# Edge lists scattered by GpSimd, the mix block moved ahead, row sums in three groups of relations

## The chip, the cores and the metric

One Trainium2 chip; the kernel runs on one core of it. The metric is the device time of one execution in microseconds (us), as the median of several runs. Engines are named PE (TensorE), DVE (VectorE), ACT (ScalarE), POOL (GpSimd) and SP (SyncE).

## The reference, cut to what matters

```python
# x [1250,1024], 20000 edges (src, dst, type in 0..7), dst sorted; all fp32
xn  = layernorm(x)
u   = xn @ root + bias
for r in range(8):                       # relational graph convolution
    sums = segment_sum(xn[src] * (type == r), dst)
    u   += (sums / max(count_r, 1)) @ weight[r]
z   = concat([u, xn]) @ w_gate + b_gate
h   = tanh(u) * z + xn * (1 - z)
mix = taylor_linear_attention(rms_norm(xn), w_q, w_kv) @ w_out     # 8 heads of 16
x   = x + h + mix
x   = x + fp4_ffn(layernorm(x))          # 1024 -> 352 -> 1024, fp4 in blocks of 16
```

## The kernel before

Rows are cut into NT = 10 tiles of 128. PE first multiplies all rows with all weights of the graph stage: 21 column blocks h (one of 384 columns for q, k, v; 16 blocks of 512 for the eight relations, two each; two for root; two for the lower half of w_gate) times 10 tiles, so NSTEP = 210 **steps** n = 10h + t. A step is `product(n)`: eight slices k of 128 input columns, three matmuls each (fp32 is made of a high and a low part, XTH/XTL and WH/WL). The finished block goes through ACT (`evacuate`, from PSUM into the tile EV) to device memory. `product` calls `beside(n, k)` after each slice k, and there everything else that PE does is placed by step number: the edge lists, the attention (mix), the summing of rows. The same step numbers place the work on the other engines, whose queues run in program order, so an instruction that waits holds up all that stands behind it on its engine. GpSimd's part in each step is `low_rows` (eight of ten steps: WL = RAW - WH, for the column block after this one; PE waits for it at the first step of a block) and then its DMAs.

A relation's result for node v is a weighted sum over v's incoming edges of rows xn[src] @ weight[r], that is of rows that `product` has stored (`relation_rows`). These rows are fetched with GpSimd's indirect DMA, 128 rows (one **item**) at a time, into a ring of four slots, and summed per tile of 128 destination nodes:

- A **plane** item holds at most one edge per destination node, so it is already aligned: DVE adds it to the sum with one SCALAR_TENSOR_TENSOR of 128x1024 (`plane`).
- A **left-over** item holds the edges that did not fit into the planes. ACT makes the high part (`left_over_hi`), DVE a one-hot matrix and the low part (`left_over`), and PE adds it with four matmuls of 512 columns (`aggregate`), in the step after the item's own, behind its last slice where the step has one such item. Only then is its slot free again.
- `finish` adds PE's sum and DVE's sum; SP stores it in u_rows (`store_sum`) and, for a later group, loads it again (`load_sum`).

Relations are taken in groups, each of which can start once its relations are multiplied. Before: group 0 is relations 0 to 4 (8 planes and 3 left-over items per tile, from step 117), group 1 is relations 5 to 7 (5 planes and 2 left-over items, from step 178). That is 180 items, 50 of them left-over.

The **lists** say which row each slot of an item holds. DVE computes a place for every edge (`edge_words`, `edge_places`, until step 19). Then for each of the 160 columns of 125 edges DVE makes three one-hot matrices and ACT two, and PE multiplies them (`list_column`, three fp16 matmuls), four columns in each of the steps 20 to 59. DVE turns the result into row numbers and weights (`list_results`).

The mix block: keys and values at steps 64 to 83 (`key_heads`; its features are made half by DVE and half by POOL, `key_features`), queries at steps 85 to 115 (`query_t`, `query_heads`, `attention_t`, `mix`). Beside steps 118 to 173 DVE quantizes the feed-forward weights (24 calls of `quantize`, three in seven steps). After step 209 come the gate matmuls and the feed-forward part. If the edges do not fit (`count_rounds`), everything is summed again in rounds (`more_rounds`).

Of the kernel before, what the change touches and what calls it, by code (L numbers as in the profile page):

```python
# [8 lines left out]
ALU = mybir.AluOpType  # L9
ACT = mybir.ActivationFunctionType  # L10
# [7 lines left out]
P = 128  # L18
N = 1250
D = 1024  # L20
# [15 lines left out]
GROUPS = ((0, 5), (5, R))  # L36
NG = len(GROUPS)
PLANES = (8, 5)
OVER = (3, 2)
# [6 lines left out]
GCB = (11, 7)  # L46
# [3 lines left out]
SW = NCOL + 2  # L50
# [42 lines left out]
LIST_FROM, LIST_EACH = 20, 4  # L93
TOTALS_AT = 76
KEYS_FROM = 64
QUERIES_FROM, QUERIES_EACH = 85, 3
AGG_FROM = (117, 178, NSTEP)
# [60 lines left out]
def gps_layer(nc, x, src, dst, edge_type_8, weight, root, bias, w_gate, b_gate, gamma, w_q, w_kv,  # L158
              w_out, ff_gate, ff_up, ff_down, out):
    with ExitStack() as ctx:  # L160
# [6 lines left out]
        def stage_tensors(*specs):  # L167
# [8 lines left out]
        qkv_d = nc.dram_tensor("qkv_rows", [NP, 3 * HID], F32).ap()  # L176
        z_d = nc.dram_tensor("gate_x_rows", [NP, D], F32).ap()
# [17 lines left out]
        iota1 = keep("iota1", [P, P], F16)  # L195
        zeros16 = keep("zeros16", [P, P], F16)
# [23 lines left out]
        unfit = keep("unfit", [P, 1], F32)  # L220
        rounds = keep("rounds", [1, 1], I32)
# [45 lines left out]
        US0, US1, XD, ZD, MD, US2 = stage_tensors(  # L267
            ("u_tile0", [P, D], F32), ("u_tile1", [P, D], F32), ("x_tile", [P, 2, D], F32),
            ("z_tile", [P, 2, D], F32), ("mix_tile", [P, 2, D], F32), ("u_tile2", [P, D], F32))
# [41 lines left out]
        dve_e = [sem(f"dve_e{j}") for j in range(5)]  # L311
# [6 lines left out]
        dve_f = [sem(f"dve_f{j}") for j in range(4)]  # L318
# [3 lines left out]
        words_ready = sem("words_ready")  # L322
        oh_dve = sem("oh_dve")
# [11 lines left out]
        f_dve = sem("f_dve")  # L335
        f_pool = sem("f_pool")
# [42 lines left out]
        pool_d = sem("pool_d")  # L379
# [18 lines left out]
        pool_x = sem("pool_x")  # L398
# [21 lines left out]
        XN = [a[:, 0:D] for a in (flat_a, flat_b)]  # L420

# [132 lines left out]
        def more_rounds(eng, body, first=None):  # L554
# [26 lines left out]
        def _(sp):  # L581
# [84 lines left out]
            for n in range(NSTEP + 1):  # L666
# [1561 lines left out]
```

## Time and profile before

| | us |
|---|---|
| median of 3 runs (lowest to highest) | 1745.39 (1743.96 to 1749.13) |
| profiled execution, its own time | 1751.03 |
| span of the profiled execution | 1749.3 |
| PE busy | 1633.5 (93%) |
| DVE busy | 995.0 (57%) |
| POOL busy | 613.0 (35%) |
| ACT busy | 498.8 (29%) |
| mean granted TensorE clock | 0.977 |

The busy time of PE is that of its matmuls, whose recorded ends overlap the next start. Idle time of the other engines costs something only where PE waits for them.

### The profile page before, as it was taken

What the parts mean: (1) busy time and instruction counts of PE and PEld (TensorE: products, weight loads), DVE (VectorE), ACT (ScalarE), POOL (GpSimd) and SP (SyncE); (2) the same over time, 40 slices, a digit from 0 to 9 for tenths busy, and PEclk for the clock granted to TensorE, in tenths of its full rate; (3) what the DMA queues carried; (4) which work ended last, traced back from release to release, by engine and by line L of the source; (5) the groups of instructions that cost most, each with busy time, mean ns of one, the idle gap of its engine ahead of it and who ended that gap; (6) DMA issues with size and microseconds to landing.
All of it is one profiled execution on the core that took longest, in us unless ns stands there. A gap on an engine that the chain in (4) does not pass through costs nothing.

```text
span 1749.3 us, 20493 instructions
## 1 busy us (share of the span) xinstructions
PE 1633.5 (93%) x7618; PEld 1290.5 (74%) x7618; DVE 995.0 (57%) x1709; ACT 498.8 (29%) x901; POOL 613.0 (35%) x523
## 2 busy tenths in 40 slices
PE   4999999999999999999999999999899869977988
PEld 4987777777777666667788787878677658866887
DVE  6544555552111433332878878884567745777885
ACT  3325555551111121212222222222211122232221
POOL 4321111124665110103555455545655641220110
PEclk8999999999999999999999999999999979987999
DMA  4321122222222222224778677777888774540001
GB/s 150 130 94 67 68 77 73 72 74 99 80 87 96 72 95 88 100 77 145 238 260 275 223 250 269 256 247 242 294 281 301 274 250 144 181 133 1 37 37 46
DMA packets 114963, 261.57 MB, mean 150 GB/s; under 512 B 18203, under 2 KB 31634, under 8 KB 114856
## 3 DMA queue, kind: packets, MB, share of 16 engines
q1 hardware_dynamic: 48568, 109.34, 18.5%
q0 software_dynamic: 27552, 82.01, 14.5%
q10 hardware_dynamic: 38736, 68.83, 10.4%
q8 instruction: 62, 1.02, 0.2%
q14 instruction: 45, 0.37, 0.1%
HBM read 192.96 MB, written 79.61 MB: 156 GB/s over the span
## 4 chain that ended last, share of the span: by engine, by line
PE 66%; DVE 16%; DMA 8%; issue 5%; ACT 3%; POOL 1%; ACTq 0%; SPq 0%; DVEq 0%; POOLq 0%
PE ps L1657 47%; DMA source_rows<-relation_rows,row_list 6%; PE ps L1872 5%; PE ps L1745 3%; DVE u_sum L1416 2%; PE ps L1904 2%; PE ps L1765 2%; PE ps L1922 1%; DVE source_rows L1400 1%; PE ps L1725 1%; DMA u_sum<-u_rows 1%; PE ps L1757 1%; ACT source_rows_hi L2048 1%; DVE wq_rows L546 1%; PE ps L1705 1%
## 5 line engine op out<-in xcount | busy, mean ns | idle before, releaser
L1657 PE MATMUL ps<-WH,XTH 128*128 128x512 f32 (+1 forms) x1680 | 681.7, 406 | 0.0
L1657 PE MATMUL ps<-WH,XTL 128*128 128x512 f32 (+1 forms) x1680 | 654.3, 389 | 0.0
L1657 PE MATMUL ps<-WL,XTH 128*128 128x512 f32 (+1 forms) x1680 | 653.7, 389 | 0.0
L814 POOL TENSOR_TENSOR WL<-RAW,WH 128x512 fp32r<-128x512 f32 (+1 forms) x184 | 241.3, 1315 | 559.9 <-ACT WH L1981 557.8
L1657 PEld LDWEIGHTS ps<-WH,XTH 128*128 128x128 f32 x1680 | 317.9, 189 | 78.1 <-issue 22.5
L1657 PEld LDWEIGHTS ps<-WH,XTL 128*128 128x128 f32 x1680 | 316.9, 189 | 65.6
L1657 PEld LDWEIGHTS ps<-WL,XTH 128*128 128x128 f32 x1680 | 318.3, 189 | 57.1 <-issue 2.4
L866 POOL DMA_INDIRECT source_rows<-relation_rows,row_list x180 | 224.2, 1245 | 263.2 <-PE ps L1765 145.2
L2003 ACT ACTIVATE EV<-ps 128x512 f32<-128x512 f32 x180 | 106.4, 591 | 452.6 <-PE ps L1657 378.1
L1416 DVE SCALAR_TENSOR_TENSOR u_sum<-source_rows,weight_list,u_sum 128x1024 f32<-128x1024 f32 x120 | 168.0, 1400 | 74.1 <-DMA source_rows<-relation_rows,row_list 67.0
L1981 ACT ACTIVATE WH<-RAW 128x512 fp32r<-128x512 f32 (+1 forms) x184 | 114.6, 624 | 140.7 <-DVE EV L1458 79.0
L1291 DVE TENSOR_SCALAR onehot<-iota,edge_words 125x128 f16<-125x128 f16 x160 | 72.1, 450 | 129.1 <-PE ps L1705 129.1
L1400 DVE SCALAR_TENSOR_TENSOR source_rows<-source_rows,weight_list,source_rows_hi 128x1024 fp32r<-128x1024 f32 x50 | 85.3, 1705 | 75.9 <-ACT source_rows_hi L2048 75.8
L1366 DVE TENSOR_TENSOR prefix<-ps,qkv_tile 128x544 f32<-128x544 f32 x40 | 29.0, 725 | 163.1 <-PE ps L1745 163.1
L2048 ACT ACTIVATE source_rows_hi<-source_rows,weight_list 128x1024 fp32r<-128x1024 f32 x50 | 57.5, 1149 | 170.6 <-DMA source_rows<-relation_rows,row_list 152.6
L2011 ACT ACTIVATE onehot<-iota,edge_words 125x82 f16<-125x82 f16 x160 | 58.1, 363 | 111.6 <-PE ps L1705 98.7
L1872 PE MATMUL ps<-WH,TH 128*128 128x512 f32 x160 | 65.3, 408 | 10.1 <-DVE TL L1516 10.1
L2012 ACT ACTIVATE onehot<-iota,edge_words 125x182 f16<-125x182 f16 x160 | 69.1, 432 | 0.0
L950 POOL TENSOR_TENSOR xf<-xf,edge_words 128x1024 f32<-128x1024 f32 x10 | 19.4, 1942 | 138.0 <-DVE xf L1566 138.0
L1350 DVE COPY values<-qkv_tile 128x128 f32<-128x128 f32 x10 | 2.4, 241 | 113.4 <-PE ps L1729 113.4
L1872 PE MATMUL ps<-WL,TH 128*128 128x512 f32 x160 | 64.2, 401 | 0.0
L1872 PE MATMUL ps<-WH,TL 128*128 128x512 f32 x160 | 64.1, 401 | 0.0
(299 smaller groups left out, 1868.8 us busy)
## 6 DMA issues: line engine op xcount, KB each, us to landing
relation_rows<-EV ACTq DMA_DIRECT2D x160, 256.0 KB, 2.0
RAW<-in_L_gnn_weight SPq DMA_DIRECT2D x128, 256.0 KB, 2.7
u_rows<-u_sum SPq DMA_DIRECT2D x20, 512.0 KB, 5.2
RAW<-in_L_gnn_w_gate SPq DMA_DIRECT2D x32, 256.0 KB, 4.7
mix_rows<-mix_rows_out ACTq DMA_DIRECT2D x10, 512.0 KB, 2.6
root_rows<-EV ACTq DMA_DIRECT2D x20, 256.0 KB, 4.5
u_sum<-u_rows SPq DMA_DIRECT2D x10, 512.0 KB, 7.6
bias_rows<-root_rows SPq DMA_DIRECT2D x10, 512.0 KB, 7.2
```

What stands on the lines that cost most here:

```text
L814: g.tensor_tensor(WL[:, h % 2, k, 0:w], RAW[:, q % 4, 0:w], WH[:, h % 2, k, 0:w].bitcast(F32), ALU.subtract).then_inc(w_lo, 1)
L866: return g.indirect_dma_start(out=XG[:, slot, :].bitcast(F32), out_offset=None, in_=y_d[group], in_offset=bass.IndirectOffsetOnAxis(ap=row ...
L1291: v.tensor_scalar(oh_src(s), iota[0:EP, 0:P], ew[0:EP, LO, col], ew[0:EP, SRC1, col], ALU.is_equal, ALU.mult)
L1400: v.scalar_tensor_tensor(rows_, rows_.bitcast(F32), weight_list[:, m.column:m.column + 1], OHI[:].bitcast(F32), ALU.mult, ALU.subtract).th ...
L1416: v.scalar_tensor_tensor(acc[:], XG[:, m.index % RING, :].bitcast(F32), weight_list[:, m.column:m.column + 1], base[:], ALU.mult, ALU.add) ...
L1657: mm = t_.matmul(ps[:, bank, 0:w], a[:, t, k, :], b[:, s, k, 0:w], start=(k == 0 and j == 0), stop=(k == KT - 1 and j == 2))
L1872: mm = t_.matmul(ps[:, 4 + 2 * s + b, :], a[:, s, k, :], w[:, h % 2, k, :], start=(k == 0 and j == 0), stop=(k == KT - 1 and j == 2))
L1981: a.activation(WH[:, h % 2, k, 0:w], raw, ACT.Copy).then_inc(w_hi, 1)
L2003: a.activation(ev_slot(s), ps[:, prod_bank(n), :], ACT.Copy).then_inc(ev, 1)
L2011: a.activation(oh_bk(s), iota[0:EP, 0:SB], ACT.Sign, bias=ew[0:EP, BQ, col])
L2012: a.activation(oh_chunk(s), iota[0:EP, 0:SW], ACT.Sign, bias=ew[0:EP, CH, col]).then_inc(oh_act, 1)
L2048: a.activation(OHI[:], XG[:, slot, :].bitcast(F32), ACT.Copy, scale=weight_list[:, m.column:m.column + 1]).then_inc(oh_hi, 1)
```

## The change

- The one-hot lists go. DVE computes for each edge a slot number (SLOT) and a word that packs source, relation and destination (WORD), and POOL writes the words with 160 indirect DMAs (125 words of 4 bytes each) into four lists in device memory, three per step from step 19; each waits for the landing of the one four before it. At step 75 the four lists are read back; DVE adds and unpacks them (`list_results`).
- The counts of edges per node and relation come from the planes by DVE reductions, and for the left-over columns from 30 matmuls of 8 columns on PE (`count_left`, steps 79 to 82).
- DVE counts the edges of each bucket directly (`bucket_totals`: three one-hots of 125x1600 and three reductions) between the edge places and the first key tile.
- The mix block moves: keys from step 20, queries from step 41. DVE makes both halves of the key features.
- Three groups: relations 0-2, 3-5, 6-7, with 7, 7, 5 planes and 1 left-over item each per tile, from steps 91, 134 and 174. That is 220 items, 30 of them left-over, and 30 sums instead of 20.
- Code for further rounds changes with it; it runs only if edges do not fit.

```diff
-GROUPS = ((0, 5), (5, R))
+GROUPS = ((0, 3), (3, 6), (6, R))
-PLANES = (8, 5)
-OVER = (3, 2)
+PLANES = (7, 7, 5)
+OVER = (1, 1, 1)
...
-LIST_FROM, LIST_EACH = 20, 4
-KEYS_FROM = 64
-QUERIES_FROM, QUERIES_EACH = 85, 3
-AGG_FROM = (117, 178, NSTEP)
+SCATTER_FROM, SCATTER_EACH = 19, 3
+KEYS_FROM = 20
+QUERIES_FROM, QUERIES_EACH = 41, 3
+LISTS_AT = 75
+COUNT_FROM = 79
+COUNTED_AT = COUNT_FROM - (-NOV // KT) + 2
+AGG_FROM = (91, 134, 174, NSTEP)
...
+            def scatter(c):
+
+                k = c % NLIST
+                pool.wait_ge(listed[k], 16 * (c // NLIST + 1))
+                g.indirect_dma_start(
+                    out=list_d[k], out_offset=bass.IndirectOffsetOnAxis(
+                        ap=ew[0:EP, SLOT, c:c + 1].bitcast(U32), axis=0),
+                    in_=ew[0:EP, WORD, c:c + 1].bitcast(I32), in_offset=None,
+                    bounds_check=P * NCOL - 1, oob_is_err=False).then_inc(listed[k], 16)
...
-                i, odd = divmod(n - KEYS_FROM, 2)
-                if 0 <= i < NT and not odd:
-                    pool.wait_ge(vt_ready, i + 1)
-                    key_features(g, i % 2, 1, f_pool)
+                if n == SCATTER_FROM:
+                    pool.wait_ge(words_ready, 1)
+                if n >= SCATTER_FROM:
+                    for c in range(c_next, min(c_next + SCATTER_EACH, EC)):
+                        scatter(c)
...
             edge_words()
             edge_places()
-            for c in range(EC):
-                list_column(c, c % 4, slice(c, c + 1), True)
-            list_results()
+            bucket_totals()
...
-                key_features(v, s, 0, f_dve)
+                for half in range(2):
+                    key_features(v, s, half, f_ready[half])
...
-                if 0 <= n - LIST_FROM < EC // LIST_EACH and k % 2 == 1:
-                    c = LIST_EACH * (n - LIST_FROM) + k // 2
-                    list_column(c, c % 4, True)
+                q = KT * (n - COUNT_FROM) + k
+                if 0 <= q < NOV:
+                    count_left(q)
```

How the change moves instructions, at three places. **PE, step 20** (WH, WL, XTH, XTL are the products' operands; onehot of L1701 to L1705 are the list's one-hots). Before, from the second slice of the step:

```order
L1657 MATMUL ps<-WL,XTH 128x512
L1657 MATMUL ps<-WH,XTL 128x512
L1701 MATMUL ps<-onehot 128x82
L1703 MATMUL ps<-onehot 128x182
L1705 MATMUL ps<-onehot 128x182
L1657 MATMUL ps<-WH,XTH 128x512
```

In the changed kernel, at the fifth slice of the same step (onehot is here the buffer with the first half of the key features):

```order
L1749 MATMUL ps<-WH,XTH 128x512
L1749 MATMUL ps<-WL,XTH 128x512
L1749 MATMUL ps<-WH,XTL 128x512
L1832 MATMUL ps<-onehot,qkv_tile 32x289 x4
L1749 MATMUL ps<-WH,XTH 128x512
```

The list's three matmuls are gone from the slices, and the first matmuls of the key heads stand in this step instead of step 64.

**DVE, behind the edge places.** Before, the last words and the first list column:

```order
L1126 TENSOR_TENSOR prefix<-prefix 125x160
L1127 TENSOR_TENSOR prefix<-prefix 125x160
L1128 TENSOR_SCALAR edge_words<-prefix 125x160
L1291 TENSOR_SCALAR onehot<-iota,edge_words 125x128
L1294 TENSOR_SCALAR onehot<-iota,edge_words 125x128
L1295 TENSOR_SCALAR onehot<-iota,edge_words 125x128
```

In the changed kernel, from the word that GpSimd waits for (L1180) to the first half of the first key tile (L440, L442):

```order
L1180 SCALAR_TENSOR_TENSOR edge_words<-prefix,unsorted 125x160
L1066 TENSOR_SCALAR edge_words<-edge_words 125x160
L1069 SCALAR_TENSOR_TENSOR edge_words<-edge_words 125x160
L1311 TENSOR_TENSOR edge_words<-edge_words 125x160
L1303 TENSOR_TENSOR onehot<-edge_words,bucket_ids 125x1600
L1314 TENSOR_REDUCE edge_totals<-onehot 125x10
L1303 TENSOR_TENSOR onehot<-edge_words,bucket_ids 125x1600
L1314 TENSOR_REDUCE edge_totals<-onehot 125x10
L1303 TENSOR_TENSOR onehot<-edge_words,bucket_ids 125x1600
L1314 TENSOR_REDUCE edge_totals<-onehot 125x10
L1438 COPY values<-qkv_tile 128x8x16
L1439 COPY values<-valid 128x8
```

The three large one-hots and their reductions stand before the key tile that PE wants in step 20.

**GpSimd, between the low halves of the weights (WL).** Before, where the 51 rows of the low halves in a run span the list stage:

```order
L855 MEMSET weight_list 128x180
L814 TENSOR_TENSOR WL<-RAW,WH 128x512 x51
L894 DMA edge_weights<-rcnt 128x80
L859 DMA weight_list<-edge_weights,weight_at 128x1 x2
L814 TENSOR_TENSOR WL<-RAW,WH 128x512
```

In the changed kernel (L829 is the low half, L908 the scatter):

```order
L872 MEMSET weight_list 128x220
L875 DMA edge_lists<-weight_list 128x220 x4
L829 TENSOR_TENSOR WL<-RAW,WH 128x512 x16
L908 DMA edge_lists<-edge_words 28160x1 x6
L829 TENSOR_TENSOR WL<-RAW,WH 128x512
L908 DMA edge_lists<-edge_words 28160x1 x3
L829 TENSOR_TENSOR WL<-RAW,WH 128x512
```

From here on three scatters stand ahead of each low half, until the 160 are done.

## Rows read from the trace of the kernel before

**Rows 1.** The page: span, busy time, the chain that ended last.
```profile
span 1749.3 us, 20493 instructions
PE 1633.5 (93%) x7618; PEld 1290.5 (74%) x7618; DVE 995.0 (57%) x1709; ACT 498.8 (29%) x901; POOL 613.0 (35%) x523
PE 66%; DVE 16%; DMA 8%; issue 5%; ACT 3%; POOL 1%; ACTq 0%; SPq 0%; DVEq 0%; POOLq 0%
```

**Rows 2.** Waits of PE: who waited for whom, us in total, times, longest.
```profile
PE ps L1765 <- DVE source_rows L1400: 30.7, 20, 3.1
```

**Rows 3.** Busy time by stretch: lists, keys, queries, both groups of sums, the rest.
```profile
core 0: us, PE busy (x) PEld busy (x) DVE busy (x) ACT busy (x) POOL busy (x), PEclk, DMA share, GB/s
136.10:397.40 261.30, 261.30 (x1443) 189.64 (x1441) 130.96 (x468) 145.51 (x384) 41.41 (x32) 1.00 0.21 74
419.70:558.20 138.50, 138.50 (x666) 99.47 (x665) 21.38 (x46) 22.08 (x36) 89.00 (x78) 1.00 0.23 78
569.20:812.90 243.70, 240.51 (x940) 166.92 (x939) 91.91 (x162) 48.66 (x83) 36.18 (x30) 1.00 0.24 86
818.40:1194.60 376.20, 364.58 (x1585) 299.02 (x1584) 296.44 (x389) 99.72 (x140) 203.00 (x161) 0.99 0.76 253
1194.60:1411.80 217.20, 198.10 (x846) 159.93 (x845) 143.38 (x124) 44.91 (x58) 121.00 (x93) 0.98 0.80 277
1411.80:1749.30 337.50, 280.46 (x1407) 243.86 (x1405) 231.05 (x321) 85.72 (x113) 60.35 (x40) 0.92 0.28 100
```

**Rows 4.** Timeline of ACT: evacuations of neighbouring steps (start, length): plain, list, left-over.
```profile
408.80 0.60 ACT L2003 ACTIVATE EV<-ps 128x512 f32<-128x512 f32 x1 [3.75 <-PE ps L1657]
414.24 0.60 ACT L2003 ACTIVATE EV<-ps 128x512 f32<-128x512 f32 x1 [3.75 <-PE ps L1657]
...
255.04 0.58 ACT L2003 ACTIVATE EV<-ps 128x512 f32<-128x512 f32 x1
261.57 0.58 ACT L2003 ACTIVATE EV<-ps 128x512 f32<-128x512 f32 x1
...
1015.72 0.60 ACT L2003 ACTIVATE EV<-ps 128x512 f32<-128x512 f32 x1 [1.88 <-PE ps L1657]
1022.07 0.60 ACT L2003 ACTIVATE EV<-ps 128x512 f32<-128x512 f32 x1 [1.48 <-PE ps L1657]
```

**Rows 5.** Timeline of PE: first matmul of step 20.
```profile
136.08 0.48 PE L1657 MATMUL ps<-WH,XTH 128*128 128x512 f32 x1
```

**Rows 6.** Timeline of DVE, edge places: carry from PE to last word, and a key tile.
```profile
116.78 0.16 DVE L1077 COPY run_carry<-ps 125x2 f32<-125x2 f32 x1 [4.80 <-PE ps L1680]
116.98 0.99 DVE L1079 TENSOR_TENSOR_SCAN prefix<-prefix,run_carry 125x160 f32<-125x160 f32 x2
118.53 0.51 DVE L1083 TENSOR_REDUCE edge_words<-prefix 125x160 f32<-125x320 f32 x1
129.09 0.24 DVE L1128 TENSOR_SCALAR edge_words<-prefix 125x160 f32<-125x160 f32 x1
...
432.20 1.29 DVE L427 TENSOR_TENSOR onehot<-qkv_tile,values 128x1088 f32<-128x1088 f32 x1
...
596.57 1.12 DVE L1368 TENSOR_REDUCE prefix<-prefix 128x34 f32<-128x544 f32 x1
```

**Rows 7.** Lines L859 (weights) and L866 (rows): indirect DMAs of GpSimd.
```profile
L859 POOL DMA_INDIRECT weight_list<-edge_weights,weight_at x50: 996/1010/2023, 421.1 to 583.8; - x50
  issue: 11.2, 46
DMA to landing us min/median/max: 2.2/2.5/4.5
...
L866 POOL DMA_INDIRECT source_rows<-relation_rows,row_list x180: 987/1072/2035, 816.0 to 1407.4; - x180
DMA to landing us min/median/max: 3.4/6.2/9.5
```

**Rows 8.** Lines of POOL, 136 to 560: busy, mean ns, idle before.
```profile
L814 POOL TENSOR_TENSOR WL<-RAW,WH 128x512 fp32r<-128x512 f32 x51 | 65.8, 1291 | 277.2 <-ACT WH L1981 277.1
```

**Rows 9.** Lines of DVE, first group of sums: busy, mean ns, idle before.
```profile
L1416 DVE SCALAR_TENSOR_TENSOR u_sum<-source_rows,weight_list,u_sum 128x1024 f32<-128x1024 f32 x70 | 95.4, 1363 | 29.5 <-DMA source_rows<-relation_rows,row_list 26.0
L1400 DVE SCALAR_TENSOR_TENSOR source_rows<-source_rows,weight_list,source_rows_hi 128x1024 fp32r<-128x1024 f32 x30 | 49.8, 1661 | 46.1 <-ACT source_rows_hi L2048 46.0
...
L1396 DVE TENSOR_SCALAR edge_one_hots<-iota,key_list 128x128 fp32r<-128x128 f16 x30 | 12.6, 420 | 0.2
L1426 DVE TENSOR_TENSOR u_sum<-ps,u_sum 128x1024 f32<-128x1024 f32 x9 | 10.9, 1215 | 0.0
```

More of the change, by code:

```diff
@@ L322, in gps_layer @@
         words_ready = sem("words_ready")
+        listed = [sem(f"listed{k}") for k in range(NLIST)]
+        lists_in = sem("lists_in")
+        left_ready = sem("left_ready")
+        left_used = sem("left_used")
+        left_ps = sem("left_ps")
         oh_dve = sem("oh_dve")
@@ L334, in gps_layer @@
         vt_ready = sem("vt_ready")
-        f_dve = sem("f_dve")
-        f_pool = sem("f_pool")
+        f_ready = [sem(f"f_ready{half}") for half in range(2)]
         key_done = sem("key_done")
@@ new lines, in edge_places @@
+                v.scalar_tensor_tensor(T(1), T(1), float(NCOL), T(3), ALU.mult, ALU.add)
+                ch.step(v.scalar_tensor_tensor(T(5), eword(BK), float(2 ** 20), T(5), ALU.mult, ALU.add))
+                v.tensor_copy(eword(WORD).bitcast(I32), T(4))
+                v.scalar_tensor_tensor(eword(SLOT).bitcast(U32), T(1), unsorted[0:EP, 1:2], T(5), ALU.add,
+                                       ALU.add).then_inc(words_ready, 1)
+            def list_results():
+                dve.wait_ge(lists_in, 16 * NLIST)
+                ch = edge_chain
+                low, high = 4 * P + NOV * R // 2, NLIST * NCOL
+                word, src, rel, key = [flat_b[:, low + NCOL * j:low + NCOL * (j + 1)] for j in range(4)]
+                none, tmp, tmp1 = [flat_a[:, high + NCOL * j:high + NCOL * (j + 1)] for j in range(3)]
+                ints = lambda w: w.bitcast(I32)
+                left = slice(NPL, NCOL)
@@ L1169, in list_results @@
                 planes = lambda w, j: w[:, PLANE0[j]:PLANE0[j] + NT * PLANES[j]].rearrange(
                     "p (t c) -> p t c", t=NT)
+                lefts = lambda j: slice(OVER0[j], OVER0[j] + NT * OVER[j])
+                group = lambda r: max(j for j in range(NG) if r >= GROUPS[j][0])
+                flat = LISTS.rearrange("p k c -> p (k c)")
+                ch.step(v.tensor_copy(flat.bitcast(F32), flat))
+                ch.step(v.tensor_reduce(word, LISTS.bitcast(F32).rearrange("p k c -> p c k"), AX.X, ALU.add))
@@ new lines, in list_results @@
+                for q in range(NOV):
+                    need(dve, left_used, q - 7)
+                    v.tensor_scalar(LEFT16[:, q % 8, :], iota1[:], key_list[:, q:q + 1], None,
+                                    ALU.is_equal).then_inc(left_ready, 1)
+                ch.step(v.tensor_scalar(none, none, 65536.0, None, ALU.mult))
+                v.tensor_tensor(src, src, none, ALU.add)
+                ch.step(v.scalar_tensor_tensor(key[:, left], key[:, left], float(NB), none[:, left], ALU.mult,
+                                               ALU.add))
@@ new lines, in list_results @@
+                ch.step(v.scalar_tensor_tensor(tmp1[:, left], rel[:, left], float(NT), key[:, left], ALU.mult,
+                                               ALU.add))
+                ch.step(v.tensor_tensor(weight_at[:], tmp1[:, left], tmp[:, left], ALU.add))
+                for r in range(R):
+                    j, same = group(r), (tmp, tmp1)[r % 2]
+                    ch.step(v.tensor_scalar(planes(same, j), planes(rel, j), float(r), None, ALU.is_equal))
+                    counted = v.tensor_reduce(rcnt[:, NT * r:NT * r + NT], planes(same, j), AX.X, ALU.add)
@@ L1672, in run_ends_t @@
                 pe.wait_ge(run_ready, 2 * level + 1)
+                if level == 0:
+                    pe.wait_ge(consts, NCONST)
+                    t_.matmul(ps[0:EP, 0, 3 * P:3 * P + 1], ones[0:EP, 0:EP], unsorted[0:EP, 0:1], start=True,
+                              stop=True)
                 t_.transpose(ps[0:NG, 0, 0:EP], run_ends[0:EP, 0:NG], ident[0:EP, 0:EP])
```

338 lines of the change are left out of this document (194 added, 144 removed).

## Prediction

> **What bounds the kernel now.** I read the page first, then the waits of PE, then busy time by stretch, then single lines. PE is busy 93% of the span and carries 66% of the chain that ended last [rows 1]; the reader is to see that no other engine comes near. PE's waits in the steps are few: the one large row is PE waiting for the low part of a left-over item, 30.7 us over 20 waits [rows 2]. So the question is how much work leaves PE's queue, and which new waits come in.
>
> The unit is the step. A plain one takes 5.44 us (evacuations at 408.80 and 414.24), one with four list columns 6.53 (255.04, 261.57), one with one left-over item 6.35 (1015.72, 1022.07) [rows 4]. By stretch: the 40 list steps take 261.3 us, the 20 key steps 138.5, the 30 query steps 243.7, steps 117 to 177 (first group of sums, 61 steps, 30 left-over items) 376.2, steps 178 to 209 (second group, 32 steps, 20 left-over items) 217.2, and all behind step 209 takes 337.5 [rows 3]. The granted clock is 1.00 up to step 115, 0.99 and 0.98 in the sums, 0.92 in the rest [rows 3]; I leave it as it is.
>
> How much the sums cost in waits: 61 plain steps are 331.8 us and 30 items at 0.91 are 27.3, which leaves 376.2 - 359.1 = 17.1 us of waiting in the first group; 32 x 5.44 + 20 x 0.91 = 192.3 leaves 24.9 us in the second. Together 42.0; rows 2 has 30.7 of it, as a wait begins in the trace only when the modelled end of the matmul before is past.
>
> **The change, part by part.**
>
> *Lists off PE.* 40 steps x (6.53 - 5.44) = -43.6 us. They stand on PE's path, and nothing but PE's own work fills these steps: PE is busy for all of the 261.3 us [rows 3].
>
> *Fewer left-over items.* 20 fewer x 0.91 = -18.2 us.
>
> *The old waits in the sums go*: -42.0, and new ones are counted below.
>
> *Mix moved.* The same matmuls in other steps: the key stretch costs 1.4 us a step above a plain one before, and will now; 0. DVE makes both halves: 1.29 us more per tile [rows 6] in a pair of steps of 13.8; hidden, except at the first tile.
>
> *The first key tile.* PE wants it behind the fifth slice of step 20. That step starts at 136.1 [rows 5], and 5/8 of 5.44 later is 139.5. DVE's side: the carry comes at 116.8, when PE reaches its place, and the last word is ready at 129.3, 12.5 us later [rows 6]. The third group adds a third scan (0.49), four more dependent operations of about 0.35 in the places, and longer products and reductions; I count 3.9 us: words at 133.2. Then `bucket_totals`: about 1 us of small operations and three pairs of a one-hot of 1600 elements and its reduction. No row has this size. A TENSOR_TENSOR of 1088 takes 1.29 us, so about 1.8 for 1600; a reduction of 320 takes 0.51, so also about 1.8 [rows 6]. Three pairs are 11.1 us: 145.3. The values and the first half take 2 us more: 147.3. PE waits 147.3 - 139.5 = +8 us, once; later tiles have a pair of steps each. Bounds: the other reduction row, 544 elements in 1.12 us [rows 6], makes three of 1600 slower by some 4 us, and with delays of 1 us by GpSimd's traffic it is 15; if my count of added operations is twice too large, 4. I take 8, as the 320-element row is contiguous like the new one.
>
> *Counting matmuls.* 30 of 8 columns. Three list matmuls with 446 columns cost (6.53 - 5.44) / 4 = 0.27 us; one tiny one lies between 0 and 0.27. I take a third, 0.09: +2.7 (0 to 8).
>
> *GpSimd's scatters.* 160 indirect DMAs, three a step from step 19 to 72. The nearest is the weight fetch, 128 words of 4 bytes: 1.01 us, with 0.24 of issue before it, landed after 2.5 (at most 4.5) [rows 7]. Each scatter waits for the fourth before it; four take 4 x 1.3 = 5.2 us, so the landing is past. Queued behind each is the low half of the weights, for which PE waits at the first step of a block. GpSimd's need over the 20 key steps is 16 x 1.29 [rows 8] + 60 x 1.3 = 99 of 138 us; over the 30 query steps 24 x 1.29 + 90 x 1.3 = 148 of 244. Hidden: 0. The lists come back at step 75, the first counting matmul is at step 79, 22 us later; the four loads (about 5 us) and some ten DVE operations before it fit.
>
> *The new sums.* Work per group as DVE must do it, at 1.36 us a plane, 1.66 + 0.42 a left-over item, 1.22 a `finish` [rows 9]. For a `quantize` I take what is left of DVE's 296.4 us in the first group [rows 3] when 80 planes (95.4 and ten more at 1.37), 49.8, 12.6 and 10.9 [rows 9] are off: 114 / 24 = 4.75 us.
> - Group 0, steps 91 to 133: PE's own time 43 x 5.44 + 9.1 = 243; DVE 95 + 21 + 12 + 6 x 4.75 = 157. Slack, but steps 91 to 99 give GpSimd two weight fetches beside two row fetches and a low half, 6 us in steps of 5.44, and the ring is cleared at its start. I take +10 (2 to 20).
> - Group 1, steps 134 to 173: PE's own time 227; DVE 95 + 21 + 12 + 18 x 4.75 = 214, which is 94%, where the first group before ran at 296.4 / 376.2 = 79% and lost 17 us in 61 steps. Low end 5, as if the rate fell with the fewer left-over items. High end: DVE's idle time of the first group, 79.8 us for 110 items or 0.73 each, stays; 214 + 58 = 272, so 45. I take +17, nearer the low end, since much of that idle time was DVE being ahead of PE.
> - Group 2, steps 174 to 209: PE's own time 205. One left-over item per 3.6 steps instead of two per 3.2. A left-over item's slot is free only when PE has added it, and the next fetch, 6.2 us to its landing and up to 9.5 [rows 7], hangs on that; before, the second of a tile blocked the first of the next. DVE has 68 + 21 + 24 + 14 for evacuations = 127. I take +4 (0 to 15).
>
> That is +31 (7 to 80). Twenty more stores and loads of sums are on SP; each load is issued two steps (group 2: 1.2) ahead of its use, and DVE, which waits for it, has the slack above; within the terms.
>
> Sum: -43.6 - 18.2 - 42.0 + 8 + 2.7 + 31 = -62 us. Against the profiled execution's own 1751.0 it gives 1689. That execution is 5.6 above the median of the runs, 1745.4, so I forecast **1683**. With all low ends it is 1745.4 - 103.8 + 11 = 1653, with all high ends 1745.4 - 103.8 + 103 = 1745.
>
> **The rivals.**
>
> *DVE becomes the bound in group 1.* For it: 94% of the stretch, and three blocks of 4.75 us in seven steps between items whose fetches want a free slot. Against it: the slack of an item is its own step and the next, about 11 us, more than one block. Group 1 then loses 45 instead of 17 and group 0 some 9 more: 1683 + 37 = 1720.
>
> *The waits nearly vanish.* For it: each fetch now moves 20000 / 220 = 91 rows instead of 111, the short left-over ones land near the least time of 3.4 us [rows 7], and one left-over item per tile frees the ring. Then the sums lose about 12 instead of 31: 1664. Against it: the quantizing beside group 1 and the first key tile remain.
>
> *The scatters hold GpSimd up (slower).* The mechanism: a scatter that takes longer than its share delays the low halves behind it, and PE stands at each tenth step from 20 to 72. The point from which it decides: keys 20.6 + 60p against 138, queries 31 + 90p against 244, so nothing is lost up to a pitch p of 1.95 us; at 2.34 (the longest of the 230 fetches, 2.04, with its issue) 23 us are lost, which leaves 1706; the whole gain is gone at 2.6; at 3.0 the loss is 120, so 1803. For it: no row shows an indirect write, and DVE works beside it all the time. Against it: the weight fetches ran beside DVE's key features and the median stayed at 1.01 us [rows 7]. The Trainium skill ("SBUF — State Buffer", "Who interferes with whom") has a rule that speaks for this rival: a DVE copy or one-scalar operation in its two-port mode holds the port pair that GpSimd needs to write descriptors, and by its section on the bandwidth-pool intuition a DMA of 0.62 us took 3.1 us beside one. By that figure as a pitch the time would be above 1803. The trace agrees only so far as single fetches take 2.02 and 2.04 us instead of 1.0 [rows 7].
>
> *It does not do what it says.* If one bucket had more left-over edges than its 128 places, a whole further round would run. Counting the reference's edges gives at most 104 in a bucket (tile 7, relations 0-2) and 87 and 65 in the other groups, so this is out. That something else keeps the order of work from moving gives 1745.
>
> **How the numbers follow.** Forecast 0.62 (its own range 1670 to 1702); DVE bound 0.17; waits vanish 0.12; scatters 0.05, of which 0.03 end slower; unchanged for any reason 0.02; slower by a loss in a place that I have not seen 0.02. The range takes in the two rivals beside the forecast up to the cut: 1658 to 1716. Within 0.3% (5 us, about what a measurement of this kernel can tell from no change) 0.02; slower 0.03 + 0.02 = 0.05; faster 0.62 + 0.17 + 0.12 + 0.02 = 0.93.
>
> **What would show it.** Right: steps 20 to 59 without 6.53 us ones outside keys and queries; one wait of PE for the first half of the key features, near 8 us, in step 20; the last product's end near 1350 (1411.8 - 62); between it and the end of the span again 337 us; row waits of PE for the low part shorter in group 2 than in group 1. Wrong: waits of PE for WL in the first half (scatters); indirect writes with a mean over 1.6 us; a stretch of steps 134 to 173 above 260 us (DVE bound); waits of PE at steps 79 to 82 for the counting one-hots; or a longer stretch behind step 209.

## The result, and the profile after

The changed kernel takes **1717.84 us** (median of 4 runs, 1716.05 to 1721.86) against 1745.18 (4 runs, 1743.96 to 1749.13): ratio 0.9843 [0.9819, 0.9867]. It is faster by 27 us where 62 were forecast, and 2 us above the range.

The page after, to be read against [rows 1]:

```profile
span 1714.3 us, 19015 instructions
PE 1576.8 (92%) x7088; PEld 1265.8 (74%) x7088; DVE 967.8 (56%) x1352; ACT 372.3 (22%) x561; POOL 823.1 (48%) x693
PE 58%; DVE 22%; DMA 8%; issue 6%; ACT 3%; POOL 3%; ACTq 0%; SPq 0%; POOLq 0%; DVEq 0%
```

PE's busy time fell by 57 us, the span by only 35, and PE's share of the chain went from 66% to 58%: work was exchanged for waits. The waits of PE after, against [rows 2] (who waited for whom: us in total, times, longest):

```profile
PE ps L1872 <- DVE source_rows L1490: 44.2, 12, 10.0
PE ps L1832 <- DVE onehot L442: 6.7, 1, 6.7
PE ps L1749 <- POOL WL L829: 2.6, 1, 2.6
```

The large row is still the left-over item's low part, but it stands for 12 long waits instead of 20 short ones. The windows after, against the last three of [rows 3]: steps 90 to 132, steps 133 to 173 (group 1 starts at 134), group 2 to the last product, the rest:

```profile
640.30:894.60 254.30, 246.26 (x1073) 202.42 (x1072) 157.30 (x155) 57.19 (x87) 164.90 (x134) 0.99 0.70 226
894.60:1152.10 257.50, 238.85 (x1026) 195.54 (x1026) 213.81 (x272) 56.41 (x85) 142.38 (x114) 0.97 0.78 259
1152.10:1381.40 229.30, 209.18 (x905) 171.75 (x903) 136.23 (x120) 38.89 (x56) 118.83 (x91) 0.96 0.72 239
1381.40:1714.30 332.90, 276.58 (x1403) 240.52 (x1402) 228.50 (x318) 85.44 (x113) 63.34 (x40) 0.92 0.27 98
```

The last product ends at 1381.4 (1411.8 before; 1350 was forecast), and 332.9 us follow. To find the rest I took the start of every step from the trace of PE and subtracted 5.44 us, and 0.91 for a left-over item; what remains is waiting, and with it the slower products behind a wait. (From 91 on it is 61.0 us where the rows of waits have 46.8: behind the wait of 10.0 us, for example, the four matmuls of the left-over item took 1.85 us instead of 0.91.) In this table the first column is the length of step 20 (a key step with no wait is 6.95), the next five are waits by steps, and "end" is that of the last product. The lower rows are experiments, told below.

| | step 20 | 91-116 | 117-133 | 134-173 | 174-177 | 178-209 | end |
|---|---|---|---|---|---|---|---|
| after | 15.9 | 6.8 | 4.5 | 25.3 | 2.7 | 21.7 | 1381.4 |
| forecast | about 15 | 10 with the next | | 17 | 4 with the next | | 1350 |
| E1 root rows without the wait | 15.4 | 8.9 | 7.1 | 22.5 | 6.1 | 0.4 | 1364.7 |
| E2 group 2 from 178 | 15.6 | 8.4 | 7.7 | 20.9 | 0.0 | 10.0 | 1366.8 |
| E3 two groups | 7.6 | 0.0 | 1.1 | 12.3 | 0.7 | 25.2 | 1372.5 |
| E4 no quantizing | 15.4 | 8.3 | 0.0 | 0.2 | 0.0 | 18.1 | 1346.2 |
| E5 changed kernel again | 15.9 | 8.9 | 7.7 | 23.5 | 5.3 | 21.0 | 1386.4 |
| E6 totals late | 7.0 | 8.5 | 4.5 | 22.9 | 5.2 | 18.8 | 1371.9 |
| E7 four weight fetches a step | 16.1 | 11.9 | 5.5 | 26.4 | 5.4 | 22.1 | 1392.3 |
| E8 four edits | 7.0 | 16.8 | 0.0 | 1.4 | 0.0 | 8.2 | 1337.8 |
| E9 groups from 95, 136, 178 | 7.0 | 6.9 | 2.8 | 2.3 | 0.1 | 10.2 | 1333.2 |
| E10 groups from 91, 134, 178 | 7.0 | 8.8 | 1.7 | 0.0 | 0.0 | 9.7 | 1331.5 |
| E11 two groups, mended | 7.0 | 0.3 | 0.0 | 0.0 | 0.0 | 22.5 | 1354.8 |
| E12 weights later | 7.0 | 0.0 | 2.3 | 0.0 | 0.1 | 13.0 | 1326.7 |
| E13 E10 again | 7.0 | 12.0 | 2.3 | 0.0 | 0.0 | 9.9 | 1335.5 |

**The first key tile.** ACT's evacuations of steps 19 and 20, 16.15 us apart, as [rows 4] are read, then DVE in between and PE's wait:

```profile
135.39 0.60 ACT L2120 ACTIVATE EV<-ps 128x512 f32<-128x512 f32 x1 [4.84 <-PE ps L1749]
151.54 0.60 ACT L2120 ACTIVATE EV<-ps 128x512 f32<-128x512 f32 x1 [15.55 <-PE ps L1749]
```

```profile
131.27 0.38 DVE L1180 SCALAR_TENSOR_TENSOR edge_words<-prefix,unsorted 125x160 uint32<-125x160 f32 x1
132.56 1.82 DVE L1303 TENSOR_TENSOR onehot<-edge_words,bucket_ids 125x1600 f32<-125x1600 f32 x1
134.41 1.82 DVE L1314 TENSOR_REDUCE edge_totals<-onehot 125x10 f32<-125x1600 f32 x1
...
145.60 0.19 DVE L442 COPY onehot<-values 128x68 f32<-128x68 f32 x1
```

```profile
138.76 0.39 PE L1749 MATMUL ps<-WH,XTL 128*128 128x512 f32 x1
145.85 2.15 PE L1832 MATMUL ps<-onehot,qkv_tile 128*32 128x289 f32 x8 [6.70 <-DVE onehot L442]
...
148.52 0.63 PE L1749 MATMUL ps<-WL,XTH 128*128 128x512 f32 x1
```

The one-hots and reductions of 1600 take 1.82 us each, as [rows 6] had let me estimate. PE stands 6.7 us, and the products behind it run slower at first (0.63 us, 0.39 ahead of it), so the step is 9.0 us longer than without the wait (E6).

**The scatters.** Line L908: least, median and longest in ns, then the idle time before it.

```profile
L908 POOL DMA_INDIRECT edge_lists<-edge_words x160: 1185/1190/2897, 132.7 to 542.0; - x160
...
  issue: 43.9, 144
  DMA edge_lists<-edge_words: 4.6, 16
...
DMA to landing us min/median/max: 2.5/2.7/5.5
```

With 197.1 us for 160, the mean is 1.23, and 0.3 of issue stands before each: a pitch of 1.5 us, below the 1.95 from which it decides. PE waited for no low half beside the scatters: its one such wait, the 2.6 us above, ends at 704.05 us, in step 100, and the last scatter began at 542.0. Steps 40 to 71 took 254.8 us, as their work did before (254.7 in steps 84 to 115).

**Group 2.** Here is what the prediction did not look at. SP's queue (issues of DMAs: start, length), then the wait behind the gap (the same row of before was 17.1 us, once):

```profile
1172.05 0.43 SPq L679 DMA_DIRECT2D u_rows<-u_sum  x1
1197.59 0.33 SPq L670 DMA_DIRECT2D bias_rows<-root_rows  x1
...
1198.91 0.43 SPq L675 DMA_DIRECT2D u_sum<-u_rows  x1
...
1220.68 0.33 SPq L670 DMA_DIRECT2D bias_rows<-root_rows  x1
```

```profile
SPq L669 <- DMA root_rows<-EV: 43.1, 2, 25.0
```

DVE's queue in the same time:

```profile
1181.59 1.22 DVE L1516 TENSOR_TENSOR u_sum<-ps,u_sum 128x1024 f32<-128x1024 f32 x1
1201.01 1.22 DVE L1521 TENSOR_TENSOR u_sum<-u_sum,bias_rows 128x1024 f32<-128x1024 f32 x1 [18.20 <-DMA bias_rows<-root_rows]
1205.35 5.45 DVE L1506 SCALAR_TENSOR_TENSOR u_sum<-source_rows,weight_list,u_sum 128x1024 f32<-128x1024 f32 x4 [3.12 <-DMA u_sum<-u_rows]
...
1225.20 1.23 DVE L1521 TENSOR_TENSOR u_sum<-u_sum,bias_rows 128x1024 f32<-128x1024 f32 x1 [8.49 <-DMA bias_rows<-root_rows]
```

And GpSimd's next row fetch, which wants a slot that DVE has read:

```profile
1207.40 1.49 POOL L887 DMA_INDIRECT source_rows<-relation_rows,row_list  x1 [20.38 <-DVE u_sum L1506]
```

In group 2 each tile's sum also gets its root rows (`load_root`), and these are products too: the second half of tile t's is made in step 180 + t. Group 2 now starts at step 174, so the load of its first tile stands in SP's queue at step 175, five steps before its data are made; SP reaches it at 1172.5 us, in step 177. SP stands 25.0 us, with the load of the next sum queued behind; DVE stands 18.20 and 3.12; GpSimd fetches nothing for 20.38; PE then loses 11.1 us in step 182.

The loss comes again for the second tile. PE had made its root rows in time (step 181 ends at 1200.1), but ACT stores them, and in ACT's queue their evacuation stands behind the high part of a left-over item, whose rows come late because GpSimd stood:

```profile
1213.11 1.15 ACT L2163 ACTIVATE source_rows_hi<-source_rows,weight_list 128x1024 fp32r<-128x1024 f32 x1 [16.56 <-DMA source_rows<-relation_rows,row_list]
1214.16 0.58 ACT L2120 ACTIVATE EV<-ps 128x512 f32<-128x512 f32 x1
1214.77 0.33 ACTq L2122 DMA_DIRECT2D root_rows<-EV  x1
```

So step 181 was evacuated at 1214.16 instead of right behind its end, SP could load its rows only at 1220.68, and DVE stood 8.49 again; PE lost 8.8 us in step 185.

### The profile page after: what moved, and what is told of

The parts are those of the page before. It is cut to its first block, busy times and chain, and to the rows that moved or that the text cites. A ratio compares the mean times of both kernels' runs of the same rounds, so it can differ in the third digit from the quotient of the medians.

```text
span 1714.3 us, 19015 instructions
## 1 busy us (share of the span) xinstructions
PE 1576.8 (92%) x7088; PEld 1265.8 (74%) x7088; DVE 967.8 (56%) x1352; ACT 372.3 (22%) x561; POOL 823.1 (48%) x693
## 3 DMA queue, kind: packets, MB, share of 16 engines
q1 hardware_dynamic: 51448, 119.83, 20.9%
## 4 chain that ended last, share of the span: by engine, by line
PE 58%; DVE 22%; DMA 8%; issue 6%; ACT 3%; POOL 3%; ACTq 0%; SPq 0%; POOLq 0%; DVEq 0%
PE ps L1749 42%; DMA source_rows<-relation_rows,row_list 5%; PE ps L1988 5%; DVE u_sum L1506 4%; PE ps L1852 3%; PE ps L2020 2%; PE ps L1832 1%; PE ps L1872 1%; DVE wq_rows L561 1%; PE ps L2038 1%; DVE wq_tmp L551 1%; DVE source_rows L1490 1%; PE ps L1864 1%; DVE wq_rows L562 1%; POOL source_rows L887 1%
## 5 line engine op out<-in xcount | busy, mean ns | idle before, releaser
L1749 PE MATMUL ps<-WH,XTH 128*128 128x512 f32 (+1 forms) x1680 | 670.6, 399 | 2.6 <-POOL WL L829 2.6
L887 POOL DMA_INDIRECT source_rows<-relation_rows,row_list x220 | 270.3, 1229 | 298.0 <-DVE u_sum L1506 145.0
L829 POOL TENSOR_TENSOR WL<-RAW,WH 128x512 fp32r<-128x512 f32 (+1 forms) x184 | 243.8, 1329 | 244.3 <-ACT WH L2098 241.6
L1506 DVE SCALAR_TENSOR_TENSOR u_sum<-source_rows,weight_list,u_sum 128x1024 f32<-128x1024 f32 x180 | 257.5, 1431 | 125.9 <-DMA source_rows<-relation_rows,row_list 104.8
L908 POOL DMA_INDIRECT edge_lists<-edge_words x160 | 197.1, 1232 | 48.5 <-issue 43.9
L1490 DVE SCALAR_TENSOR_TENSOR source_rows<-source_rows,weight_list,source_rows_hi 128x1024 fp32r<-128x1024 f32 x30 | 50.2, 1673 | 89.8 <-ACT source_rows_hi L2163 89.8
L1872 PE MATMUL ps<-source_rows_hi,edge_one_hots 128*128 128x512 f32 x60 | 22.0, 450 | 44.2 <-DVE source_rows L1490 44.2
L2163 ACT ACTIVATE source_rows_hi<-source_rows,weight_list 128x1024 fp32r<-128x1024 f32 x30 | 34.4, 1147 | 108.6 <-DMA source_rows<-relation_rows,row_list 102.6
L1852 PE MATMUL ps<-key_value,q_t 32*128 32x289 f32 x160 | 48.6, 422 | 3.2
```

The costliest lines, as they stand in the source:

```text
L829: g.tensor_tensor(WL[:, h % 2, k, 0:w], RAW[:, q % 4, 0:w], WH[:, h % 2, k, 0:w].bitcast(F32), ALU.subtract).then_inc(w_lo, 1)
L887: return g.indirect_dma_start(out=XG[:, slot, :].bitcast(F32), out_offset=None, in_=y_d[group], in_offset=bass.IndirectOffsetOnAxis(ap=row ...
L908: g.indirect_dma_start(out=list_d[k], out_offset=bass.IndirectOffsetOnAxis(ap=ew[0:EP, SLOT, c:c + 1].bitcast(U32), axis=0), in_=ew[0:EP, ...
L1490: v.scalar_tensor_tensor(rows_, rows_.bitcast(F32), weight_list[:, m.column:m.column + 1], OHI[:].bitcast(F32), ALU.mult, ALU.subtract).th ...
L1506: v.scalar_tensor_tensor(acc[:], XG[:, m.index % RING, :].bitcast(F32), weight_list[:, m.column:m.column + 1], base[:], ALU.mult, ALU.add) ...
L1749: mm = t_.matmul(ps[:, bank, 0:w], a[:, t, k, :], b[:, s, k, 0:w], start=(k == 0 and j == 0), stop=(k == KT - 1 and j == 2))
```

## The experiments

Ratios are against the kernel before, run beside each on the same chip. The batches are E1 to E4, E5 to E8, E9 to E11, and E12 with E13. In the diffs `...` marks lines left out.

**E1, root rows without their wait.** It adds rows of the mix in place of the root rows, so that part of the sum is other data.

```diff
-                    n = NT * (H_ROOT + b) + t
-                    sp.wait_ge(ev_out[n % 4], ev_stores(n))
-                sp.dma_start(BIASB[:], root_d[rows(t), :]).then_inc(root_in, 16)
+                    sp.wait_ge(mix_out[b], 16 * NT // 2)
+                sp.dma_start(BIASB[:], mix_d[rows(t), :]).then_inc(root_in, 16)
```

> The rows that SP loads into bias_rows for the last group are taken from mix_rows (stored since step 72) instead of root_rows; so the output leaves out the root product. Theory A (SP stands before the root rows: tile 0 of group 2 asks for them in step 175, but step 180 makes them): PE's waits in steps 174 to 209 fall from 24.5 us to under 7, and the time from 1717.8 to about 1700. Rival B (DVE comes out of group 1 too late, being 94% busy there, and the waits of group 2 are what is left of it): both stay, time 1715 to 1720.

1700.56 us, 0.9707 [0.9657, 0.9758]; 0.4 us of waits from step 178 on instead of 21.7. PE's row fell:

```profile
PE ps L1871 <- DVE source_rows L1489: 25.7, 10, 6.3
```

Group 1's waits (22.5) stayed, and so did the 6.1 us of steps 174 to 177 (5.3 in E5). So the root rows make the waits from step 178 on, and only these: of the 24.4 us that group 2 lost, some 21. The rest, at step 175, is gone in E2 and in E4.

**E2, group 2 from step 178**, with groups 0 and 1 where they were.

```diff
-AGG_FROM = (91, 134, 174, NSTEP)
+AGG_FROM = (91, 134, 178, NSTEP)
+AGG_TO = (134, 174, NSTEP)      # where the tiles of a group are spread to
...
-                step = AGG_FROM[g] + (each * t + at) * (AGG_FROM[g + 1] - AGG_FROM[g]) // (each * NT)
+                step = AGG_FROM[g] + (each * t + at) * (AGG_TO[g] - AGG_FROM[g]) // (each * NT)
```

> Group 2 (relations 6-7) starts at step 178 instead of 174; groups 0 and 1 keep their steps. Theory A: tile 0 is finished in step 181, when its root rows are there or nearly; waits of steps 174 to 209 fall from 24.5 to 8 us or less, since 60 items in 32 steps are still fewer a step than the 70 of the kernel before; time about 1701. Rival B says the same of the first waits, as DVE gets four steps to catch up, but not of e1. A third reading (the rate of the last group decides): waits as in the kernel before, 20 to 25 us, time 1718.

1703.5 us, 0.9717 [0.9668, 0.9766]: a start four steps later more than halves the loss (24.4 to 10.0, where 8 or less was expected). SP still stands 17.0 us for the first root rows, but DVE only 4.0. What the other 10 us are was not tried; 8 to 13 us stand there in every later run with three groups whose last starts at 178.

**E3, two groups**: the new lists and the moved mix alone, sums as before.

```diff
-GROUPS = ((0, 3), (3, 6), (6, R))
-PLANES = (7, 7, 5)
-OVER = (1, 1, 1)
+GROUPS = ((0, 5), (5, R))
+PLANES = (8, 5)
+OVER = (3, 2)
...
-AGG_FROM = (91, 134, 174, NSTEP)
+AGG_FROM = (117, 178, NSTEP)
```

> The new lists and the moved mix alone: two groups (0-4, 5-7) with 8 and 5 planes, 3 and 2 left-over items per tile, from steps 117 and 178, as in the kernel before. From the changed kernel's terms: 1745.2 - 43.6 (list columns) + 6 (first key tile, with one group less) + 50 x 0.15 (counting matmuls) and the sums as before, so 1715. If the three groups are worth what I forecast (more than 20 us), it is above 1725.

1712.95 us, 0.9774 [0.9729, 0.9819]. The lists and the mix give what the whole change gives (1719.27 us, 0.9823, in E5): three groups, placed as they are, were worth nothing.

**E4, no quantizing.** DVE's 24 `quantize` become a copy of 16 columns; the feed-forward part then works on unquantized weights.

```diff
-                        quantize(v, ch, WQI[:, m, :], WQT[:], WQS).then_inc(wq_done, 1)
+                        v.tensor_copy(WQT[:, 0:16], WQI[:, m, 0:16]).then_inc(wq_done, 1)
```

> DVE's 24 quantize calls become one short copy each; the feed-forward weights go through unquantized, which is the part left out. Theory A: group 1's waits (25.3 us in steps 134 to 173) fall to under 8, those of group 2 stay at 18 to 25, because SP waits for a product and not for DVE; time about 1700. Rival B: both fall, to under 8 each, time about 1683.

1685.04 us, 0.9626 [0.958, 0.9671]. Group 1's waits go from 25.3 to 0.2, those from step 178 on stay at 18.1, and DVE stands as long for the root rows:

```profile
1169.40 1.22 DVE L1521 TENSOR_TENSOR u_sum<-u_sum,bias_rows 128x1024 f32<-128x1024 f32 x1 [18.99 <-DMA bias_rows<-root_rows]
```

Two causes, then: the quantizing for group 1 and the root rows for steps 178 on. The time is 15 us below the 1700 expected and near the rival's 1683, though the rival's waits did not come out: the quantizing had also made the waits of steps 117 to 133 (4.5, 7.7 in E5) and 174 to 177 (2.7, 5.3 in E5), which are gone here.

**E5, the changed kernel again**, for comparison in its batch.

> The changed kernel itself, unedited, beside the next three on one chip. It should stand at 0.984 of the kernel before, as measured first (0.9819 to 0.9867); the other three are read against it.

1719.27 us, 0.9823 [0.9784, 0.9863]. The waits repeat within 3.2 us.

**E6, bucket totals late**: behind the last query tile, in the buffer `prefix`.

```diff
             edge_places()
-            bucket_totals()
...
                 attention(t)
+            bucket_totals()
             list_results()
```

> The bucket totals (three one-hots of 1600 elements and their reductions) move from ahead of the first key tile to behind the last query tile, where DVE waits for the lists; they use the other scratch buffer. If step 20's extra 9 us (15.9 against 6.8) is DVE's 11 us of bucket totals, step 20 falls to 7 us or so and the time by 9 us against e5. Rival (the longer chain of edge places is the cause): step 20 stays above 12 us.

1708.66 us, 0.9772 [0.9732, 0.9812]; ACT's evacuations of steps 19 and 20 are 7.18 us apart instead of 16.15:

```profile
135.79 0.60 ACT L2120 ACTIVATE EV<-ps 128x512 f32<-128x512 f32 x1 [4.84 <-PE ps L1749]
...
142.97 0.60 ACT L2120 ACTIVATE EV<-ps 128x512 f32<-128x512 f32 x1 [6.58 <-PE ps L1749]
```

**E7, four weight fetches a step** instead of two, to have them over before group 0.

```diff
-                    for q in range(w_next, min(w_next + 2, NOV)):
+                    for q in range(w_next, min(w_next + 4, NOV)):
...
-                    w_next = min(w_next + 2, NOV)
+                    w_next = min(w_next + 4, NOV)
```

> GpSimd fetches the left-over weights four a step from step 85 instead of two, so it is done at step 92 instead of 99. If the 6.8 us wait in steps 100 and 101 is GpSimd with too much to do beside the first items (two weight fetches, two row fetches and a low half in a step), it falls below 1 us, and the time by 6 us against e5. Rival (the clearing of the ring and the short lead at the start of group 0): it stays, or moves to step 93.

1724.03 us, 0.9855 [0.9817, 0.9893]. Missed: 11.9 us in steps 91 to 116, no less than in E5, now at steps 92 and 96 instead of 100.

**E8, four edits together**: group 2 from step 178, E6, E7 and a spread of the quantizing. Unlike E2, group 1 is stretched here to the start of group 2, 44 steps instead of 40; so it is in E10, E12 and E13 (E9: 42).

```diff
-AGG_FROM = (91, 134, 174, NSTEP)
-QUANT_FROM, QUANT_STEPS = 118, 7
+AGG_FROM = (91, 134, 178, NSTEP)
+QUANT_FROM, QUANT_STEPS = 92, 11
...
-in (2, 3, 5):
+in (2, 5, 8):
```

> All together: totals late (-9), four weight fetches a step (-6), group 2 from step 178 with group 1 stretched to 44 steps, and the quantize calls spread over steps 92 to 180, three in eleven steps instead of three in seven. Theory: DVE is no longer above 85% in any stretch and SP no longer stands before the root rows; waits in steps 91 to 209 fall from 61 us to 20, so together -50 against e5: about 1667. If either cause is only half of it, the time stays above 1685.

1678.33 us, 0.9598 [0.9561, 0.9635]. Group 1's waits are nearly gone (1.4), but 16.8 us stand at the start (E7 alone 11.9, E5 8.9), and the time is 11 us above the 1667 expected. E7's edit and the quantizing that now begins at step 92 were not parted there.

**E9 and E10, without E7's edit**, quantizing from step 100, three in ten steps; E9 with groups from 95, 136, 178, E10 from 91, 134, 178.

```diff
-QUANT_FROM, QUANT_STEPS = 118, 7
+QUANT_FROM, QUANT_STEPS = 100, 10
```

> As e8, but two weight fetches a step again, group 0 from step 95 (95, 136, 178) and the quantize calls from step 100, three in ten steps. Reading: the 17 us that e8 lost in steps 92 to 97 are GpSimd behind with fetches, the clearing of the ring and the first items, since e7 only moved the wait of steps 100 and 101 to 92 to 97 and made it larger. With four steps more, waits in steps 91 to 116 are under 4 us and the time is 12 us below e8: 0.953 of the kernel before. If what decides is the rate of the items (41 steps instead of 43), they stay above 8.

> As e9, but groups from steps 91, 134, 178. GpSimd's pile-up at the start as in the changed kernel: 7 to 9 us in steps 100 and 101, so 5 to 8 us above e9 and 0.956 to 0.958 of the kernel before.

E9: 1669.94 us, 0.9545 [0.9519, 0.9571]. E10: 1669.63 us, 0.9539 [0.9513, 0.9565]. The two are equal; that E10 would be slower was a miss, and so was E9's 6.9 us at the start where under 4 was expected. A start four steps later only moved the first wait, from step 100 to step 104.

**E11, two groups mended** in the same way, from 114 and 178.

> Two groups as in the kernel before (from steps 114 and 178), with the new lists, the moved mix, the late totals and the spread quantize calls: what three groups are worth once both waits are mended. PE has 20 more left-over items (18.2 us) and the old waits of the last group (25 us, one left-over item blocking the next); so 30 to 40 us above e9, 0.973 to 0.977 of the kernel before. If three groups are worth nothing, it equals e9.

1695.75 us, 0.9697 [0.9668, 0.9726]: 26 us above E9, where 30 to 40 was expected. So three groups are worth 26 us once the waits around them are mended: 20 left-over items (18.2), 12.8 less waiting in group 2 and 3 for fewer counting matmuls, against some 10 more at the start (E10's row and E11's). These add up to some 24, and the last products' ends are 23.3 us apart.

**E12, weights later; E13, E10 again.** What held up step 100 was still open. In E10 GpSimd has no idle time but issue from 649 to 704 us: two weight fetches, two row fetches and a low half take it 6.6 to 7.7 us in a step of 5.44.

```diff
-                    for q in range(w_next, min(w_next + 2, NOV)):
+                    w_to = min(w_next + 2, OVER0[1] - NPL) if n < 105 else min(w_next + 1, NOV)
+                    for q in range(w_next, w_to):
```

> As the best kernel so far (groups from 91, 134, 178, bucket totals late, quantizing from step 100), but GpSimd fetches only group 0's ten columns of weights at two per step from step 85; the other twenty follow one per step from step 105. Theory P (GpSimd's pace: in steps 92 to 99 two weight fetches, two row fetches and a low half take 6.5 to 7.5 us of a 5.4 us step, and GpSimd never idles from 649 to 704 us, so rows come later from step to step until PE stands at step 100): GpSimd has idle time before steps 95 to 100, the wait at steps 100 and 101 (7.3 us in the kernel without this edit) goes to under 1 us, steps 91 to 116 lose at most 2 us beyond their own work instead of 8.8, and the time is 6 to 8 us lower than the run of the unedited kernel in this batch (ratio about 0.950 against 0.954). Theory Q (the wait comes from the ring's clearing and from rows that land late while the first sums and their stores begin, whatever GpSimd's pace): steps 91 to 116 keep 6 us or more, and the time stays within 2 us of the unedited kernel.

> The unedited kernel for comparison in this batch (groups from 91, 134, 178, bucket totals late, quantizing from step 100, two weight fetches per step from step 85). Both theories: ratio 0.954, 7 to 9 us of waits in steps 91 to 116, most of it at step 100.

E12: **1662.65 us** (1658.43 to 1664.02), 0.9496 [0.9464, 0.9528]; E13: 1669.94 us, 0.9547 [0.9515, 0.958]. The intervals of the ratios overlap a little, but the single times do not (E13: 1668.68 to 1674.75), and the traces are clear: no wait in steps 91 to 116 against 12.0 (8.8 in E10, 7 to 9 expected). Window of POOL from 640 to 700 (us, busy with instructions, PEclk, DMA share, GB/s), E12:

```profile
640.00:700.00 60.00, 34.41 (x28) 1.00 0.73 241
```

and E13:

```profile
640.00:700.00 60.00, 47.59 (x40) 0.97 0.60 186
```

GpSimd runs 12 instructions fewer, and more moves (241 against 186 GB/s): from 640 to 704 us 21 row fetches start instead of 16, and GpSimd now stands waiting for a free slot in between (5.86 and 6.07 us). E12 is the fastest kernel here: 5.0% below the kernel before, where the changed kernel is 1.6 to 1.8% below (E5).

## Why the prediction was right or wrong

Right as worked out:
- *Lists off PE, fewer items, no effect of the moved queries.* Steps 20 to 209 contain no list columns and 30 items at 0.91.
- *Scatters hidden.* The pitch was 1.5 us against my 1.3, the point of decision 1.95. The rule of the Trainium skill ("SBUF — State Buffer", "Who interferes with whom") made me look at this. The trace bears it out only in part: 78 of the 160 scatters had no DVE operation beside them, and none of these took over 1.22 us; all 13 that took longer had one. For nine of these (1.45 to 2.28 us) it was a copy of the key features, and 11 more with a copy beside took no longer than the rest. The three longest of the others (1.77 to 2.90) ran beside the one-hots and reductions of 1600, which are not copies. It came too seldom to cost anything here.
- *First key tile.* +8; step 20 took 15.93 us and takes 6.95 without the wait (E6), so +9.0, at the place named. The two are made up differently: the words were ready at 131.7 us, not 133.2, and PE stood 6.7; the other 2.3 are mostly the slower matmuls behind the wait, which I had not counted.
- *Group 0, in part by luck.* +10; 11.3 measured. Only 6.8 of it, in steps 100 and 101, came by the mechanism named (GpSimd's fetches beside the low half), as E12 showed. The other 4.5, in steps 126 and 130, came from the quantizing (E4: 0.0), where I had written "Slack" for DVE.

Off in size:
- *Counting matmuls.* +2.7; steps 79 to 82 took 6.6 us each, 1.17 above a plain one for 8 matmuls: 0.15 each, 4.6 together.
- *Group 1.* +17 (5 to 45); 25.3. In steps 134 to 173 DVE was busy for 208.9 us (214 forecast), the stretch took 252 us, under the 260 that I had named for a DVE bound, and E4 shows the quantizing to be the cause. I had taken 94% of the stretch as a rate, where the waits stand in single steps (147: 5.5, 167: 7.9), while 18 blocks of quantizing (5.5 us each by its ten lines, 93.0 us for 17 calls, not 4.75) stand three in seven steps. With the 24 blocks spread from step 100 on, three in ten steps, 12 of them in steps 134 to 173, the waits were gone (E10: 0.0). Whether the spacing, the smaller number or the stretching of group 1 from 40 to 44 steps did it was not tried apart.

**The step that failed** is group 2's: "I take +4 (0 to 15)", and with it the sentence that SP's stores and loads are "within the terms". It measured 24.4, outside its bounds, some 21 of them from the root rows (E1: 0.4 from step 178 on instead of 21.7) and the rest from the quantizing ahead of it (E4; a later start removes it too, E2). I counted items per step, where the rate did fall, and saw each load of SP as a duration. I did not ask when the data of `load_root` exist. What I had named as a sign, waits for the low part shorter in group 2 than in group 1, came out the other way: the longest, 10.0, is in group 2. The row was there before too (17.1 us on SP, once, with a start at 178; DVE stood only 1.5 us for it), so a look at SP's waits would have shown it. With the start at 174 SP stood 43.1 us for it, with 178 in the changed kernel 17.4 (E2).

The terms are off by 20.4 (group 2), 8.3 (group 1), 1.3 (group 0), 1.0 (key tile) and 1.9 (counting), together 33; the part behind the last product was 4.6 shorter than before. The profiled execution came out at 1716.05 against 1689, 27 more, which leaves 1.3 unexplained. Another 7 us come from the medians: I took the before's 5.6 over to the changed kernel, whose profiled execution was 1.8 below its median. That difference between executions is not explained.

The prediction put the difference between its 42.0 us of waits and the 30.7 of [rows 2] down to the modelled ends alone. These give 0.16 us a wait (0.39 against a pitch of 0.23), so 3 us for 20 waits. The other 8 are no idle time but matmuls that start further apart behind a wait, as the 0.63 us ones in step 20 do; in the changed kernel they make 12 of the 61 us.

The rival "DVE becomes the bound in group 1" named the right engine and place, with 45 where 25 came. That its total of 1720 lies 2 us from the measured time, nearer than the forecast, is luck: it had nothing for the root rows. "The waits nearly vanish" was out for this kernel, yet E12 shows that they can: 15.4 us in all.

## What to carry to other kernels

When a group of work is moved ahead, list for each of its loads the step that makes the data, and look at every queue in which that load stands in order: an early load whose data come late stops all loads behind it. Stores are in such a queue too: here a late row fetch held up ACT, and with it the store of rows that were long made. Waits between a few engines with much slack came here from what met in one step, not from the mean load; count the work of each engine in the worst steps, and spread it before removing it. A wait at one point can undo a gain elsewhere, so compare waits stage by stage, from the starts of steps, rather than totals.

## What the runs showed of the hardware

- An indirect write of 125 words took GpSimd 1.19 us in the median (1.23 mean, 2.90 longest) and 0.3 us to the next, and landed after 2.7 us; with no DVE operation beside it, none of 78 took over 1.22; an indirect read of 128 words took 1.01 [rows 7].
- A tiny matmul of 8 columns in between fp32 products cost PE 0.15 us, more than half of the 0.27 that one of the lists' wider matmuls cost.
- A wait of 6.7 us cost 9: the granted clock was 1.00 when PE stopped at 139.2, fell while it stood (0.85 in the mean up to 145.8), was 0.50 from 145.8 to 150.0 (the lower of its two levels, 1.2 GHz) and 1.00 again from 152.0. Products of 512 columns took 0.63 us instead of 0.39 until about 150.2. The stretch with the wait in it:

```profile
135.40:151.40 16.00, 9.30 (x35) 6.15 (x34) 11.49 (x11) 0.59 (x1) 7.43 (x6) 0.79 0.09 18
```

- Fetching faster moved the wait to earlier steps and did not make it smaller (E7: 11.9 against 8.9); fetching later removed it (E12). GpSimd's queue in the start-up stretch was the scarce thing.
